# Second attention of a two-layer kernel: scores from three bf16 parts as six products in 64-row strips, operands stacked by 0/1 matmuls

## The chip, the cores and the metric

The kernel runs on one core of a Trainium2 chip. The metric is the device time of one execution in microseconds (us). TensorE (PE in the profile, PEld its weight loads) multiplies, VectorE (DVE), ScalarE (ACT) and GpSimd (POOL) do the rest, SyncE (SP) issues DMAs.

## The reference

Two layers, each an attention block and a feed-forward block with adaptive layer norm, on x of 1 x 2048 x 128. Only the second attention changes:

```python
q = (x @ Wqa @ Wqb).reshape(b, s, H, D)            # H = 16 heads, D = 8, s = 2048
kv = (x @ Wkva @ Wkvb).reshape(b, s, KVH, D, 2)    # KVH = 4 groups of keys and values
k, v = (kv[..., 0], kv[..., 1])
q = _rope(q); k = _rope(k)
k = jnp.repeat(k, g, axis=2); v = jnp.repeat(v, g, axis=2)
scores = jnp.einsum('bqhd,bkhd->bhqk', q, k) * scale
scores = jnp.where(causal[None, None], -jnp.inf, scores)
w = jax.nn.softmax(scores, axis=-1)
out = jnp.einsum('bhqk,bkhd->bqhd', w, v).reshape(b, s, E)
return out @ Wout + bout
```

## The kernel before

Each engine has its own program; semaphores join them. The 2048 tokens are four chunks c of 512 (`CW`), each four tiles of 128. The order in time is: first attention, routed experts, layer norm `norm(2)`, the second attention, `norm(3)`, the second experts.

**Operands.** A head has only 8 dimensions. To keep precision with bf16 matmuls, q and k are cut into three bf16 parts, and all nine products of parts are contracted at once: 9 x 8 = 72 rows (`KROWS`), plus two rows that subtract the row maximum, in a 128-row operand padded with zeros and ones. Per chunk the tensor engine makes latents (`latents`, L881 and L882), then q, k and v from them (`heads`, L888 to L895); the vector engine applies rope and splits (`rope_and_split`, L1726 to L1746: 14 operations); SyncE writes the parts to DRAM (`q_parts`, `k_parts`) and 18 DMAs per chunk read them back into the stacked form (`stack`, L482 and L485; chunks 2 and 3 from GpSimd's queue). Two GpSimd memsets fill the padding: L647 right after the first attention, L654 once the residual of the experts is added (`x2_ready`).

**Items and steps.** The work is 16 items n, one per chunk c = n // 4 and key group g (four heads). Two passes run over each item. The maxima pass makes scores with queries as rows, in "slots": a slot is one PSUM bank filled by TensorE (L927, and L930 and L931 for a diagonal tile and its mask) and read by a maximum on VectorE (L1766); banks 0, 1 and 7 rotate, so TensorE waits for the reader of three slots before. The main pass goes in steps (n, j), one per key tile j: 160 steps, 4, 8, 12 or 16 per item by chunk; the last four of each item are diagonal ones with fewer columns. A step is `sum_scores` for two pairs of heads (L968 to L971, transposed scores with the maximum subtracted), two exponentials on ScalarE (L1289) and `values` (L983, four fp32 matmuls side by side in 32 columns each), which runs one step behind. `attention_schedule` deals the slots out among the steps, so that an item's maxima are known before its first step; the slots of items 0 and 1 come before step 0. After an item VectorE copies its sum out (`copy_out`, L1754), and slots "out", "turned" and "product" finish it.

```python
                beside = SLOTS[s + 1]
                if j == 0:
                    pe.wait_ge(ld_nm[n % G1], 32 * (n // G1 + 1))
                cuts = [0, (len(beside) + 3) // 4, (len(beside) + 1) // 2, len(beside)]
                sum_scores(s, 0)
                for what in beside[cuts[0]:cuts[1]]:
                    slot(what)
                sum_scores(s, 1)
                for what in beside[cuts[1]:cuts[2]]:
                    slot(what)
                if s >= 1:
                    values(s - 1)
                for what in beside[cuts[2]:cuts[3]]:
                    slot(what)
```

## Time and profile before

| | us |
|---|---|
| median of 3 runs | 1316.51 (1315.25 to 1318.33) |
| profiled execution, span | 1317.5 |
| TensorE busy | 1166.7 (89%) |
| VectorE busy | 1046.4 (79%) |
| ScalarE busy | 776.6 (59%) |
| GpSimd busy | 43.9 (3%) |

The profile gives the profiled execution no other time than its span, from the first to the last instruction. It lies 1.0 us (0.08%) above the median. Busy shares are averages over stages with different limits, and matmuls overlap one another, so an engine's limit is read from the starts of its instructions in one stage.

### The profile page before, as it was taken

Reading aid. Unit: us, or ns where it says so; the run is one execution under the profiler, and the core shown is the slowest. Engines: PE = TensorE matmul, PEld = TensorE weight load, DVE = VectorE, ACT = ScalarE, POOL = GpSimd, SP = SyncE. Lnnn points to the kernel's source line nnn. Section 1 sums busy time; section 2 is a strip of 40 time slices with the busy share of each in tenths; the row PEclk is TensorE's granted clock in tenths of the full one; section 3 lists DMA queues with packets and bytes.
Section 4 is the critical chain, followed back from the end, with each engine's and each line's share of the span. In section 5 each row is a group of like instructions: output and inputs, shape, how many; then the busy total and the mean of one; then the engine's idle time right before and its main releaser. Section 6 shows DMA issues by size and latency. Waiting matters only on the chain.

```text
span 1317.5 us, 17710 instructions
## 1 busy us (share of the span) xinstructions
PE 1166.7 (89%) x6249; PEld 680.9 (52%) x6249; DVE 1046.4 (79%) x2018; ACT 776.6 (59%) x1151; POOL 43.9 (3%) x45
## 2 busy tenths in 40 slices
PE   3888647999999855779999999999998799999998
PEld 2333333666666512345444443443332688888886
DVE  4699998788888883879899889888851688888885
ACT  1635414899999710135555656566676566666664
POOL 0000020000000040140000000000000000000000
PEclk9898767899999956589999999999999699999999
DMA  5000000000000214551000000000000121111001
GB/s 161 0 0 1 0 24 17 16 17 16 18 14 1 78 35 79 72 78 16 2 2 2 1 1 2 1 1 1 1 1 1 45 102 56 56 56 56 0 1 33
DMA packets 38169, 35.02 MB, mean 27 GB/s; under 512 B 15162, under 2 KB 33530, under 8 KB 36810
## 3 DMA queue, kind: packets, MB, share of 16 engines
q1 hardware_dynamic: 36082, 31.12, 9.0%
q0 software_dynamic: 2016, 2.96, 1.7%
q8 instruction: 44, 0.72, 0.2%
q14 instruction: 27, 0.22, 0.1%
HBM read 30.85 MB, written 3.08 MB: 26 GB/s over the span
## 4 chain that ended last, share of the span: by engine, by line
PE 61%; DVE 26%; ACT 6%; issue 3%; DMA 3%; SPq 1%; DVEq 0%; ACTq 0%
PE ps L822 10%; PE ps L823 10%; PE ps L824 10%; PE ps L983 9%; DVE arena_a L1766 7%; PE ps L927 7%; PE ps L971 6%; DVE arena_b L1472 3%; DVE mv L1377 2%; PE ps L839 1%; ACT arena_b L1222 1%; DMA arena_a<-q_parts 1%; PE ps L693 1%; DMA arena_a<-arena_a 1%; DVE xn L1384 1%
## 5 line engine op out<-in xcount | busy, mean ns | idle before, releaser
L1766 DVE TENSOR_REDUCE arena_a<-ps 128x1 f32<-128x512 f32 (+3 forms) x560 | 344.4, 668 | 73.2 <-PE ps L931 46.3
L1289 ACT ACTIVATE arena_b<-ps 128x1024 f32<-128x1024 f32 (+3 forms) x320 | 274.0, 894 | 191.8 <-PE ps L971 169.6
L822 PE MATMUL ps<-parts 128*128 128x512 f32 x640 | 273.2, 427 | 7.1 <-DVE parts L1688 4.2
L823 PE MATMUL ps<-parts 128*128 128x512 f32 x640 | 251.5, 393 | 0.0
L824 PE MATMUL ps<-parts 128*128 128x512 f32 x640 | 251.2, 392 | 0.0
L927 PE MATMUL ps<-arena_b,arena_a 128*128 128x512 bf16 (+3 forms) x576 | 190.4, 354 | 6.3 <-DVE arena_a L1766 4.9
L971 PE MATMUL ps<-arena_a,arena_b 128*128 128x512 bf16 (+3 forms) x576 | 163.2, 348 | 0.7 <-ACT arena_b L1289 0.3
L983 PE MATMUL ps<-arena_b 128*32 128x512 f32 (+3 forms) x1280 | 151.1, 544 | 2.5 <-DVE arena_b L1754 2.2
L822 PEld LDWEIGHTS ps<-parts 128*128 128x128 f32 x640 | 122.0, 191 | 36.8 <-DVE parts L1688 9.7
L824 PEld LDWEIGHTS ps<-parts 128*128 128x128 f32 x640 | 121.0, 189 | 26.4
L823 PEld LDWEIGHTS ps<-parts 128*128 128x128 f32 x640 | 121.4, 190 | 22.4
L1867 DVE TENSOR_TENSOR arena_b<-ps,arena_b 128x512 f32<-128x512 f32 x128 | 88.3, 690 | 55.4 <-PE ps L824 51.6
L927 PEld LDWEIGHTS ps<-arena_b,arena_a 128*128 128x128 bf16 x576 | 52.8, 99 | 143.0 <-DVE arena_a L1766 119.0
L1312 ACT ACTIVATE arena_b<-ps 128x512 f32<-128x512 f32 x128 | 76.6, 599 | 84.5 <-PE ps L824 84.0
L1677 DVE TENSOR_TENSOR arena_b<-ps,arena_b 128x512 f32<-128x512 f32 x128 | 88.1, 689 | 35.2 <-ACT arena_b L1226 34.8
L1688 DVE TENSOR_TENSOR parts<-arena_b,parts 128x512 fp32r<-128x512 f32 x128 | 87.6, 685 | 1.2
L1872 DVE TENSOR_TENSOR parts<-arena_b,parts 128x512 fp32r<-128x512 f32 x128 | 87.3, 682 | 0.1
L1226 ACT ACTIVATE arena_b<-arena_b 128x512 f32<-128x512 f32 x128 | 80.7, 631 | 3.6
L1222 ACT ACTIVATE arena_b<-ps 128x512 f32<-128x512 f32 x128 | 74.9, 585 | 9.2 <-PE ps L824 9.1
L1316 ACT ACTIVATE parts<-arena_b 128x512 fp32r<-128x512 f32 x128 | 79.9, 624 | 0.4 <-DVE arena_b L1867 0.4
L971 PEld LDWEIGHTS ps<-arena_a,arena_b 128*128 128x128 bf16 x576 | 53.3, 99 | 35.0 <-ACT arena_b L1289 13.4
L930 PE MATMUL ps<-arena_b,arena_a 128*128 128x128 bf16 x256 | 53.8, 236 | 12.0 <-DMA arena_a<-q_parts 12.0
(274 smaller groups left out, 1445.3 us busy)
## 6 DMA issues: line engine op xcount, KB each, us to landing
arena_b<-expert_weights SPq DMA_DIRECT2D x7, 1024.0 KB, 6.7
arena_a<-q_parts SPq DMA_DIRECT2D x18, 128.0 KB
arena_a<-q_parts POOLq DMA_DIRECT2D x18, 128.0 KB, 5.9
wslot<-in_L_ffn_up_w SPq DMA_DIRECT2D x8, 256.0 KB, 3.1
wslot<-in_L_ffn_down_w SPq DMA_DIRECT2D x8, 256.0 KB, 3.3
wslot<-in_L_ffn_w_gate SPq DMA_DIRECT2D x8, 256.0 KB, 2.9
wslot<-in_L_ffn_w_up SPq DMA_DIRECT2D x8, 256.0 KB, 3.4
wslot<-in_L_ffn_w_down SPq DMA_DIRECT2D x8, 256.0 KB, 3.8
```

Of the source, the lines that this page charges most:

```text
L822: mm(bank, w(0), x(0), start=start, stop=False)
L823: mm(bank, w(0), x(1), start=False, stop=False)
L824: return mm(bank, w(1), x(0), start=False, stop=stop)
L927: last = mm(b[:, at_:at_ + full], q, kst[:, g, u * CW:u * CW + full], start=True, stop=True)
L971: last = mm(ps[:, 2 + i, full:CW], k, q[:, full:CW], start=True, stop=True)
L983: last = mm(ps[32 * i:32 * i + 32, 6, off:CW], vaug[:, j, g, :], probs[:, s % 2, i, off:CW], start=(j == 0), stop=(j == TPC * c + TPC - 1) ...
L1222: a(relu[:, k % NBUF, :], ps[:, k % 2, :], ACT.Relu).then_inc(moe_relu, 1)
L1289: a(probs[:, s % 2, 2 * pair:2 * pair + 2, off:CW], ps[:, 2 + 2 * pair:4 + 2 * pair, off:CW], ACT.Exp, scale=scale).then_inc(p2_exp, 1)
L1677: v.tensor_tensor(prod0[:, k % NBUF, :], ps[:, 2 + k % 2, :], sq0[:, k % NBUF, :], ALU.mult)\
L1688: v.tensor_tensor(hid0[:, k % NBUF, 1, :], prod0[:, k % NBUF, :], hid0[:, k % NBUF, 0, :].bitcast(F32), ALU.subtract).then_inc(moe_lo, 1)
L1766: v.tensor_reduce(mx[:, n % 2, i:i + fit, t % TPC, u], b[:, 0:fit * w].rearrange("p (h k) -> p h k", k=w), AX_X, ALU.max)\
L1867: v.tensor_tensor(prod1[:, k % NBUF, :], ps[:, 2 + k % 2, :], silg[:, k % 2, :], ALU.mult)\
```

## The change

- Six products of the nine are kept (`PRODUCTS`), so 48 rows and two for the maximum: 50 (`MROWS`). Two heads stand in one operand, in rows 0 to 49 and 64 to 113 (`STRIP` = 64), and each matmul of scores uses one strip.
- Projection weights are merged before the experts (`wq`, `wkv`): two transposes and two matmuls on TensorE, four copies on ScalarE. `queries`, `keys` and `values_all` take the normed x directly. All keys are roped and split once, four chunks in four bands of 32 partitions (`rope_k`).
- The DRAM trip is gone. A stacked operand is three matmuls by a 0/1 matrix (`stack`, L922) and a ScalarE copy (`stack_copy`, L1320 or L1322): 12 such before the first slot, 36 among the slots.
- Diagonal slots: instead of 11 slots per item on the diagonal, 12 ("diag" with one 512-column mask for four tiles, "below3", "below12").
- Both large GpSimd memsets are gone. GpSimd does the small weight copies and the bias addition on 128 x 2048 that VectorE did at L1718. `copy_out` moves to ScalarE. The maxima chain has one operation less.

```diff
+PRODUCTS = ((0, 0), (0, 1), (1, 0), (1, 1), (0, 2), (2, 0))
+KROWS = len(PRODUCTS) * HD
+MROWS = KROWS + 2
+STRIP = 64
...
+        blocks = [("scores", t, u) for t in range(TPC * c, TPC * c + TPC) for u in range(c)]
+        blocks += [("diag", 0, 0), ("below3", 0, 0), ("below12", 0, 0)]
+        for k, (what, t, u) in enumerate(blocks):
+            scores += [(what, n, t, u, i) for i in range(HPG)]
+            if c < NC - 1 and (len(blocks) - 1 - k) < HPG - 1:
+                scores.append(("stack", -1, c + 1, n % G1, k + HPG - 1 - len(blocks)))
...
-            nc.gpsimd.memset(kst[64:P, :, :], 1.0).then_inc(kones, 1)
-            nc.gpsimd.memset(qst[64:P].rearrange("p c h t -> p (c h t)").bitcast(F32), 0.0).then_inc(qzero, 1)
+            g.tensor_tensor(xt[:, :, :], xt[:, :, :], bo1[:, :].unsqueeze(1).broadcast_to([P, NT, D]), ALU.add)\
+                .then_inc(bias_ready, 1)
...
+            def stack(e, b):
+                c, g, kind = STACKS[e]
+                r = slice(0, P) if kind else slice(32 * c, 32 * c + 32)
+                for a in range(NPART):
+                    last = mm(b, spread[r, g, kind, a, :], (q3[:, c, a, :] if kind else k3[r, a, :]),
+                              start=(a == 0), stop=(a == NPART - 1))
+                return last
...
+                    r = slice(STRIP * (i % 2), STRIP * (i % 2) + KROWS)
+                    def pairs(at_, tq, k0, kw, stop=True):
+                        return mm(b[:, at_:at_ + kw], qst[r, g, tq // TPC, i // 2, tq % TPC * P:(tq % TPC + 1) * P], kst[r, g, k0:k0 + kw],
+                                  start=True, stop=stop, skip_group_check=not stop)
...
-                for i in (2 * pair, 2 * pair + 1):
-                    k = kst[:, g, j * P:(j + 1) * P]
-                    q = qst[:, c, HPG * g + i, :]
+                def part(i, lo, hi, stop):
+                    r = slice(STRIP * i, STRIP * i + MROWS)
+                    return mm(ps[:, 2 + 2 * pair + i, lo:hi], kst[r, g, j * P:(j + 1) * P],
+                              qst[r, g, c, pair, lo:hi], start=True, stop=stop)
...
+            keys(NC - 1)
+            queries(2)
+            stacks_before()
+            for what in SLOTS[0][:NITEM0]:
+                slot(what)
+            queries(3)
+            values_all()
+            for what in SLOTS[0][NITEM0:]:
+                slot(what)
...
+                    slots(beside[cut:] if pair else beside[:cut])
+                if s >= 1 and STEPS[s - 1][0] != n:
+                    copy_out(n - 1, s)
```

What stands on TensorE where the second attention begins, before the change: transposes of the norm (L674), then projections (L888 to L895 are `heads`, L881 and L882 `latents`), then the first slots.

```order
L674 MATMUL ps<-ident,xn 128x128 x4
L888 MATMUL ps<-arena_b,wqb 128x512
L889 MATMUL ps<-arena_b,wqb 128x512
L892 MATMUL ps<-arena_b,wkk 32x512
L893 MATMUL ps<-arena_b,wkk 32x512
L895 MATMUL ps<-wkk,arena_b 128x32 x4
L881 MATMUL ps<-hT,wqa 64x512
L882 MATMUL ps<-hT,wkva 32x512
```

And after it, from the third chunk's transposes on (L891 and L892 are `queries`, L897 and L899 `keys`, L922 `stack`, L961 and L974 a slot's scores and its mask):

```order
L675 MATMUL ps<-ident,xn 128x128 x4
L891 MATMUL ps<-hT,wq 128x512
L892 MATMUL ps<-hT,wq 128x512
L897 MATMUL ps<-hT,wkv 32x512
L899 MATMUL ps<-hT,wkv 32x512
L675 MATMUL ps<-ident,xn 128x128 x4
L897 MATMUL ps<-hT,wkv 32x512
L899 MATMUL ps<-hT,wkv 32x512
L922 MATMUL ps<-arena_a,arena_b 128x512 x36
L961 MATMUL ps<-arena_a 128x128 x4
L974 MATMUL ps<-maskqk,identb 128x512
```

The projections depend on nothing but the normed x now, and 36 stacking matmuls stand between them and the first slot.

A full step on TensorE, before (L971 `sum_scores`, L927 a slot, L983 `values`):

```order
L927 MATMUL ps<-arena_b,arena_a 128x512
L971 MATMUL ps<-arena_a,arena_b 128x512 x2
L927 MATMUL ps<-arena_b,arena_a 128x512 x2
L971 MATMUL ps<-arena_a,arena_b 128x512 x2
L927 MATMUL ps<-arena_b,arena_a 128x512
L983 MATMUL ps<-arena_b 32x512 x4
```

and after (L1010 `sum_scores`, L961 a slot, L1032 `values`):

```order
L961 MATMUL ps<-arena_a 128x512 x2
L1010 MATMUL ps<-arena_a 128x512 x2
L961 MATMUL ps<-arena_a 128x512
L1010 MATMUL ps<-arena_a 128x512 x2
L961 MATMUL ps<-arena_a 128x512
L1032 MATMUL ps<-arena_b 32x512 x4
```

The count is the same; each L1010 pair and each pair of neighbouring L961 now lies in different strips.

ScalarE in the first steps after the change (L1359 are the exponentials, L1320 and L1322 copies of stacked operands):

```order
L1359 ACTIVATE arena_b<-ps 128x1024
L1320 ACTIVATE arena_a<-ps 128x512
L1359 ACTIVATE arena_b<-ps 128x1024
L1359 ACTIVATE arena_b<-ps 128x2x384
L1322 ACTIVATE arena_a<-ps,onerow 128x512
L1359 ACTIVATE arena_b<-ps 128x2x384
L1359 ACTIVATE arena_b<-ps 128x2x256
L1320 ACTIVATE arena_a<-ps 128x512
```

Before, exponentials alone stood there; the copies come in between. Per item there are now 4, 3, 2, 1 stacks in chunk 0, 4, 4, 2, 2 in chunk 1 and 3, 3, 3, 0 in chunk 2.

## Rows read from the trace of the kernel before

**Rows 1.** The page: busy time by engine, share of the span, instructions.

```profile
PE 1166.7 (89%) x6249; PEld 680.9 (52%) x6249; DVE 1046.4 (79%) x2018; ACT 776.6 (59%) x1151; POOL 43.9 (3%) x45
```

**Rows 2.** Windows: busy time by engine (instructions), granted TensorE clock, DMA.

```profile
480.00:493.00 13.00, 12.54 (x23) 4.08 (x21) 7.86 (x13) 1.05 (x2) 0.00 (x0) 0.50 0.00 0
825.00:850.00 25.00, 24.87 (x193) 10.20 (x191) 21.94 (x41) 15.36 (x19) 0.00 (x0) 1.00 0.00 1
```

**Rows 3.** Timeline, GpSimd and VectorE: start, duration, operation, idle time before.

```profile
185.79 6.92 POOL L647 MEMSET arena_b<- 64x8192 bf16 x1 [184.95 <-DVE xt L1494]
187.09 5.65 DVE L1377 TENSOR_SCALAR mv<-mv 128x4 f32<-128x4 f32 x1
464.41 13.75 POOL L654 MEMSET arena_a<- 64x16384 f32 x1 [269.55 <-DVE xt L1494]
465.65 12.54 DVE L1377 TENSOR_SCALAR mv<-mv 128x4 f32<-128x4 f32 x1
480.63 2.29 DVE L1718 TENSOR_TENSOR xt<-xt,bo 128x2048 f32<-128x2048 f32 x1
```

**Rows 4.** Timeline of the start of the second attention.

```profile
464.79 1.97 PE L881 MATMUL ps<-hT,wqa 128*64 128x512 f32 x2
479.42 1.12 PE L674 MATMUL ps<-ident,xn 128*128 128x128 f32 x4 [10.82 <-DVE xn L1384]
482.34 1.91 PE L889 MATMUL ps<-arena_b,wqb 64*128 64x512 f32 x2
484.18 1.91 PE L892 MATMUL ps<-arena_b,wkk 32*32 32x512 f32 x2
485.88 1.91 PE L893 MATMUL ps<-arena_b,wkk 32*32 32x512 f32 x2
487.93 0.69 DVE L1726 TENSOR_TENSOR arena_b<-ps,arena_a 128x512 f32<-128x512 f32 x1 [5.00 <-PE ps L893]
495.24 0.67 DVE L1746 TENSOR_TENSOR arena_b<-arena_b 32x512 bf16<-32x512 f32 x1
523.90 0.27 PE L930 MATMUL ps<-arena_b,arena_a 128*128 128x128 bf16 x1 [11.99 <-DMA arena_a<-q_parts]
556.82 0.26 PE L968 MATMUL ps<-arena_a,arena_b 128*128 128x128 bf16 x1 [4.04 <-DVE arena_b L1729]
```

**Rows 5.** Timeline of one full step in chunk 2, on three engines.

```profile
828.10 1.06 PE L983 MATMUL ps<-arena_b 128*32 128x512 f32 x8
829.10 0.60 PE L927 MATMUL ps<-arena_b,arena_a 128*128 128x512 bf16 x2
829.52 2.48 DVE L1766 TENSOR_REDUCE arena_a<-ps 128x1 f32<-128x512 f32 x4 [0.48 <-PE ps L927]
829.54 0.59 PE L971 MATMUL ps<-arena_a,arena_b 128*128 128x512 bf16 x2
...
830.17 1.94 ACT L1289 ACTIVATE arena_b<-ps 128x1024 f32<-128x1024 f32 x2 [0.89 <-PE ps L971]
830.62 0.38 PE L927 MATMUL ps<-arena_b,arena_a 128*128 128x512 bf16 x1
830.92 1.06 PE L983 MATMUL ps<-arena_b 128*32 128x512 f32 x8
```

**Rows 6.** Timeline: `copy_out` after the last item of chunks 0 to 2, then items 14 and 15.

```profile
618.17 0.68 DVE L1754 COPY arena_b<-ps 128x512 f32<-128x512 f32 x1
711.21 0.68 DVE L1754 COPY arena_b<-ps 128x512 f32<-128x512 f32 x1
850.01 0.68 DVE L1754 COPY arena_b<-ps 128x512 f32<-128x512 f32 x1
980.80 0.69 DVE L1754 COPY arena_b<-ps 128x512 f32<-128x512 f32 x1 [3.83 <-PE ps L983]
1011.97 0.69 DVE L1754 COPY arena_b<-ps 128x512 f32<-128x512 f32 x1 [28.89 <-PE ps L983]
```

**Rows 7.** Groups by line: a ScalarE copy-like operation from PSUM, 512 columns.

```profile
L1312 ACT ACTIVATE arena_b<-ps 128x512 f32<-128x512 f32 x128 | 76.6, 599 | 84.5 <-PE ps L824 84.0
```

More of the change, by code:

```diff
@@ L78, in attention_schedule @@
     scores.append(("maxima", NITEM - 1))
-    end = {n: max(k for k, x in enumerate(scores) if x[1] == n and x[0] == "scores") + 1 for n in range(NITEM)}
+    end = {n: max(k for k, x in enumerate(scores) if x[1] == n and x[0] != "maxima") + 1 for n in range(NITEM)}
     slots = [scores[:end[1]]]
@@ L414, in adaln_two_layers, with slot_before @@
         STEPS, SLOTS, LAST_SLOTS = attention_schedule()
-        FIRST = [SLOTS[0][:len(SLOTS[0]) // 2], SLOTS[0][len(SLOTS[0]) // 2:]]
         NFIRST = len(SLOTS[0])
+        PRE = 3 * G1
+        STACKS = [(c, g, kind) for c in range(NC) for g in range(G1) for kind in range(3)]
         def slot_bank(m):
             return m % 2 if m < NFIRST else (0, 1, 7)[m % 3]
-        def slot_free(m):
-            return m - 1 if m < NFIRST else max(NFIRST, m - 2)
-        READ = {what: m + 1 for m, what in enumerate([x for part in SLOTS for x in part] + LAST_SLOTS)}
+        ORDER = [x for part in SLOTS for x in part] + LAST_SLOTS
+        READ = {}
+        for what in ORDER:
+            READ[what] = 1 + sum(1 for x in READ if (x[0] == "stack") == (what[0] == "stack"))
+        def slot_before(m):
+            same = [k for k in range(m) if slot_bank(k) == slot_bank(m)]
+            return ORDER[same[-1]] if same else None
+        NITEM0 = min(k for k, x in enumerate(SLOTS[0]) if x[1] == 1 or x[0] == "maxima")
         HALF = GP * NC
@@ L899, in after_turn, with stacks_before @@
             def after_turn(c):
-                if c >= 2:
-                    heads(c - 2)
                 if c >= 1:
-                    latents(c - 1)
+                    if c <= 2:
+                        queries(c - 1)
+                    keys(c - 1)
+            def stack(e, b):
[5 more added lines that the diff above has]
+                return last
+            def stacks_before():
+                pe.wait_ge(ld_e, 16)
+                pe.wait_ge(ksplit_ready, 1)
+                for e in range(PRE):
+                    if e == 1:
+                        pe.wait_ge(split_ready, 1)
+                    if e >= 2:
+                        pe.wait_ge(stack_ready, e - 1)
+                    stack(e, ps[:, 6 + e % 2, :]).then_inc(stack_mm, 1)
             slot_at = [0]
@@ L961, in sum_scores @@
                     pe.wait_ge(p2_exp, 2 * s + pair - 1)
[L962 to L971 removed]
+                full = off + P if j >= TPC * c else off
+                def part(i, lo, hi, stop):
+                    r = slice(STRIP * i, STRIP * i + MROWS)
+                    return mm(ps[:, 2 + 2 * pair + i, lo:hi], kst[r, g, j * P:(j + 1) * P],
+                              qst[r, g, c, pair, lo:hi], start=True, stop=stop)
+                if full > off:
+                    for i in range(2):
+                        part(i, off, full, False)
+                    for i in range(2):
+                        last = mm(ps[:, 2 + 2 * pair + i, off:full], identb[:, :], maskkq[:, :], start=False, stop=True)
+                if full < CW:
+                    for i in range(2):
+                        last = part(i, full, CW, True)
                 last.then_inc(p2_mm, 1)
@@ L1749, in copy_out, with rope_q @@
-            def copy_out(n, steps):
-                dve.wait_ge(pv_mm, steps)
-                if n >= 2:
-                    dve.wait_ge(slot_read, READ["out", n - 2])
-                v.tensor_copy(oT[:, n % 2, :], ps[:, 6, :]).then_inc(o_copy, 1)
+            chain(v.memset(mx, -BIG))
+            dve.wait_ge(ld_rope, 48)
+            def rope_q(c):
+                b, bank = c % 2, 4 - 2 * (c % 2)
+                dve.wait_ge(q_mm, c + 1)
+                if c == 1:
+                    dve.wait_ge(ksplit_ready, 1)
+                elif c >= 2:
+                    dve.wait_ge(split_ready, c - 1)
+                v.tensor_tensor(ra[:, b, :], ps[:, bank, :], ropec[:, chunk(c)], ALU.mult).then_inc(rope_done, 1)
+                v.tensor_tensor(rb[:, b, :], ps[:, bank + 1, :], ropes[:, chunk(c)], ALU.mult).then_inc(rope_done, 1)
+                dve.wait_ge(rope_done, 2 * c + 2)
+                chain(v.tensor_tensor(ra[:, b, :], ra[:, b, :], rb[:, b, :], ALU.add))
+                split(q3[:, c], ra[:, b, :]).then_inc(split_ready, 1)
```

418 lines of the change are left out of this document (210 added, 208 removed).

## The prediction, as it was put on record

> **What bounds the kernel now.** The page first: TensorE is busy 89% of the span, VectorE 79% [rows 1]. Only the stretch from about 456 to 1013 us belongs to the second attention, so I read the windows of it next. From 825 to 850 TensorE shows 24.87 of 25 us, VectorE 21.94, ScalarE 15.36, at full clock (2.4 GHz); from 480 to 493, at the start, the clock is at half (1.2 GHz), VectorE is busy 7.86 of 13 us and ScalarE 1.05 [rows 2]. Two stages, then, with different limits.
>
> **The steps.** The timeline of one full step settles what limits them [rows 5]. `values` starts at 828.10 and again at 830.92: 2.82 us per step. In between TensorE never stops: 1.00 us for `values`, then eight bf16 matmuls of 512 columns (four slots, four of `sum_scores`) from 829.10 to 830.62 for seven of them, 0.217 us each, and 0.30 us from the start of the last to the next `values`, that is 0.085 beyond its 0.217. VectorE needs 2.48 us for four maxima and then waits (0.48 before); ScalarE needs 1.94 and waits 0.89. TensorE is the bound, VectorE is next at 88% of the step, ScalarE third at 69%.
>
> **The start.** The timelines of GpSimd and VectorE, side by side, show an operation on 4 elements, L1377, lasting 12.54 us while GpSimd's memset L654 runs, and ending with it (478.19 against 478.16); its twin at 187.09 lasts 5.65 us beside L647 [rows 3]. Unhindered it takes 0.17. After it comes a chain through projection, rope, store and reload: TensorE's first slot waits 11.99 us for `q_parts`, and the first step begins at 556.82 [rows 4].
>
> **The change part by part.** The sum is made against the profiled 1317.5 us, which is the median within 0.1%.
>
> *First memset gone:* 5.65 - 0.17 = -5.5 us. This VectorE chain feeds the routing before the experts, and TensorE waits for it, so it counts in full. Bounds -4 (six small GpSimd copies now come there; they are priced by nothing here) and -7. The merging of weights falls where TensorE and ScalarE wait for the routing on VectorE: nothing; without that cover some 4 us.
>
> *The start anew*, from 465.7 us, where L1377 stalled. It now passes in 0.17, so the 12.4 us is part of what follows. TensorE needs (at half clock, as rows 4 show for such matmuls) three times `queries` and four times `keys`, with the transposes of two chunks between them (1.1 us, L674). L889 to L892 gives 1.84 us for a matmul, L892 to L893 1.70. From 464.8: queries 3.7, keys 3.4, transposes 1.1, queries 3.7, keys 3.4, transposes 1.1, keys twice 6.8, together 23.2: 488.0. `rope_k` is half of the 14 operations between 487.93 and 495.91 [rows 4], 4.1 us: 492. Rope of q0 lies under the projections, that of q1 under the stacks. The bias addition on GpSimd (2.29 us on VectorE at L1718) blocks, if it blocks like a memset, operations that wait for keys anyway: nothing. Twelve stacks are 36 matmuls: at half clock 0.43 each, 15.5 us; at full clock the two banks and the copy (0.60, [rows 7]) bind, about 0.85 per stack, 10: 502 to 507.5. First slots (12 and 3 stacks): VectorE 12 x 0.6 = 7, or TensorE cold 11: 510 to 518.5. The last queries, rope of q2 and `values_all` are waited for one after another: 8 to 12: 518 to 530. Second slots 8 to 10, rope of q3 until its banks are read 1.3: step 0 begins between 527 and 541.5 against 556.8 in the trace. I take the middle, -23 us, bounds -15 and, with TensorE warm from 480 on, -34.
>
> *The steps.* Four terms per step, if two matmuls in different strips run together:
> - `sum_scores`, full step: four matmuls become two pairs: 0.87 - 0.43 = -0.43 us.
> - A diagonal step gains as much less by its columns, but its masks need all 128 rows, so a pair of heads goes from strips to the full array and back. A change of form is read off `values`: 0.085 us in, and 1.00 - 4 x 0.217 = 0.13 in and out together with its drain, so about 0.09. The gain in a diagonal step is eaten by this: nothing.
> - A full slot is still one matmul; only neighbours in different strips can overlap. A "diag" slot gets two changes of form, +0.2 us, four per item.
> - A stack slot adds 3 x 0.217 + 0.2 = 0.85 us on TensorE, 36 of them 31 us, on ScalarE 0.60, 36 of them 22, none on VectorE.
>
> A full step then is 1.09 + 0.43 + 4 x (0.11 to 0.217) = 1.95 to 2.4 us on TensorE, 2.4 to 2.48 on VectorE, 1.94 on ScalarE. VectorE becomes the bound at 2.45: -0.38 per full step. By chunks, against the copy-outs [rows 6]:
> - Chunk 3, 162 us: 36 full steps with slots by 0.38 = -14; item 15 without slots goes from TensorE (31.2 us) to ScalarE, 1.94 per full step against 2.09: -2; -17 with a `copy_out` less on VectorE.
> - Chunk 2, 138.8 us: 32 full steps, -12, nine stacks displace as much VectorE work as they add: -11.
> - Chunk 1, 93.0 us: 16 full steps would give -6, but 12 stacks (10 us) and 16 "diag" slots fall on TensorE: 24 to 29 us per item against 23.3: +5.
> - Chunk 0, 61.4 us from step 0, with an item and a half under cold clock and a late reload: TensorE 57: -3.
>
> Together -26 us. Bounds: -50 if changes of form cost nothing and neighbours always overlap, +15 if strips don't run together.
>
> *Sum:* -5.5 - 23 - 26 = -54.5, so 1317.5 - 54.5 = **1263 us**.
>
> The Trainium skill has a rule against this. Its page "TensorEngine Tiling (Array Packing)", section Tiling Modes, says that changing the mode, not only the tile, drains the array. The row agrees: 0.085 us into `values`; the other way, the page "TensorE: Matmul & The Clock Gate" (Part 2) puts a drain at about 128 cycles, by my estimate 0.053 us, and over some 450 changes of form the sum would be about 15 us lower. The first page also says that row tiles work in parallel, which no row here shows.
>
> **The rivals.**
> 1. *Strips don't overlap.* Nothing in the trace has two matmuls in different row strips. Then full steps stay at 2.82, and stacks (31 us) and diag slots (16 x 0.8) load TensorE where chunks 0 and 1 have no slack: +10 to +15 on the steps instead of -26: 1300 us. Chance 0.14.
> 2. *Slower than before: the clock falls.* The granted clock was at half from 480 to 493 [rows 2] while TensorE worked without a pause in matmuls of 64*128 and 32*32, 1.84 and 1.70 us each [rows 4]; it was at full in the stage of 128*128 and four-wide `values` [rows 2]. The new steps use 50 rows per matmul. At half clock a full step costs 2.0 + 0.17 + 0.87 + 0.9 = 3.9 us on TensorE, 1.1 above now; 96 of them +105, diagonal ones +1 each, +64, minus 34 at the start: about 1450. It decides once it holds in a fifth of the steps. Against it: `values` fills its four column strips at once and takes 41% of the step. Chance 0.07.
> 3. *Stacks stall the slots.* A bank with a stack is free only when ScalarE, in its order, has passed an exponential and copied. TensorE queues everything behind it: `sum_scores`, `values`. At 0.5 to 0.9 us for each of 36, 18 to 32 us: 1288. For: ScalarE's order ties copies to exponentials. Against: it is idle 31% of a step. Chance 0.13.
> 4. *Better than forecast:* full clock from the start and cheap changes of form, -34 and -50: about 1228. Chance 0.12.
>
> **How the numbers follow.** The forecast (1240 to 1280) has 0.54. The range holds 1, 3 and most of 4: 1230 to 1300; outside are 0.07 for rival 2 and about 0.12 at the two ends. A measurement of this kernel tells 0.2% (2.6 us) from no change. Slower: rival 2, and 0.01 for others, 0.08; the same 0.02; faster 0.90.
>
> **What would show it.** L1377 at 0.17 us in both norms. Step 0 begins 61 to 76 us after the third L1377 of `norm(2)`, not 91. Starts of an L1010 pair a few ns apart, in full steps 2.45 us from one L1032 to the next, with VectorE gapless and TensorE waiting for it. Chunk 1 no faster than before. The prediction is wrong if L1010 starts are 0.217 apart (rival 1), if the granted clock is below 1.00 in the steps (rival 2), or if TensorE waits for L1320 (rival 3).

## The result, and the profile after

The changed kernel takes **1297.78 us** (median of four, 1295.01 to 1299.13) against 1315.88 (1310.24 to 1318.33) beside it: ratio 0.9885, 95% interval 0.9842 to 0.9927. The direction is as forecast. The time is inside the range (1230 to 1300) by 2.2 us, and that is luck: a start that came earlier than forecast stands against steps that came out longer. Of the 54.5 us forecast, 18.1 are there between the medians and 24.3 between the profiled spans (1317.5 and 1293.2). The spans are used below because only a profile can be split into stages; that of before, 1317.5, is above the median of its times even without what a time holds beyond the span, so it is one of its longer executions. In the page, VectorE lost and ScalarE gained; TensorE did not lose anything [rows 1]:

```profile
PE 1171.0 (91%) x6178; PEld 626.5 (48%) x6191; DVE 1010.3 (78%) x1975; ACT 808.4 (63%) x1208; POOL 8.0 (1%) x14
```

Timeline of the changed kernel, from the first norm after the first layer to the first step (start, duration, engine, line, operation; in brackets the idle time before it and what ended it):

```profile
186.74 0.53 DVE L1451 TENSOR_SCALAR mv<-mv 128x4 f32<-128x4 f32 x1
...
458.87 0.17 DVE L1451 TENSOR_SCALAR mv<-mv 128x4 f32<-128x4 f32 x1
...
461.58 4.52 POOL L658 TENSOR_TENSOR xt<-xt,bo 128x2048 f32<-128x2048 f32 x1 [272.89 <-DVE xn L1458]
...
463.13 3.52 DVE L1794 TENSOR_TENSOR arena_b<-arena_b 128x512 f32<-128x512 f32 x1
...
476.00 0.74 PE L922 MATMUL ps<-arena_a,arena_b 32*128 32x512 bf16 x2 [2.66 <-DVE arena_a L1802]
...
519.81 0.29 PE L1010 MATMUL ps<-arena_a 50*128 50x128 bf16 x2 [2.63 <-issue]
```

L1451 is the old L1377. It takes 0.53 and 0.17 us where it took 5.65 and 12.54 [rows 3]: both memset stalls are gone, but for 0.36 us of the first, which ended together with a GpSimd memset of 1.80 us that was left in (L637, 185.44 to 187.24). From the third L1451 of the norm to step 0 it is 519.81 - 458.87 = 60.9 us, forecast 61 to 76, before 91.2. Step 0 begins 37.0 us earlier than at 556.82 [rows 4], forecast 28.5 with the first memset. The first part did better than forecast.

The steps did not. ScalarE's `copy_out` after the last item of chunks 0 to 3:

```profile
584.85 0.60 ACT L1348 ACTIVATE arena_b<-ps 128x512 f32<-128x512 f32 x1
...
687.26 0.60 ACT L1348 ACTIVATE arena_b<-ps 128x512 f32<-128x512 f32 x1
...
835.69 0.60 ACT L1348 ACTIVATE arena_b<-ps 128x512 f32<-128x512 f32 x1
...
987.80 0.60 ACT L1348 ACTIVATE arena_b<-ps 128x512 f32<-128x512 f32 x1 [0.55 <-PE ps L1032]
```

Against [rows 6], from step 0 on, in us:

| chunk | before | forecast | after | 64-row strips (below) |
|---|---|---|---|---|
| 0 | 61.4 | 58 | 65.0 | 63.6 |
| 1 | 93.0 | 98 | 102.4 | 102.3 |
| 2 | 138.8 | 128 | 148.4 | 132.4 |
| 3 | 162.0 | 145 | 152.1 | 152.0 |
| all | 455.2 | 429 | 468.0 | 450.4 |

So the steps take 13 us more than before instead of 26 less; -37 + 13 = -24 is the whole change. A full step in chunk 3 is what the forecast said (timeline of TensorE, then of the other two engines):

```profile
891.90 1.06 PE L1032 MATMUL ps<-arena_b 128*32 128x512 f32 x8
892.90 0.39 PE L961 MATMUL ps<-arena_a 48*128 48x512 bf16 x2
893.13 0.38 PE L1010 MATMUL ps<-arena_a 50*128 50x512 bf16 x2
893.38 0.39 PE L961 MATMUL ps<-arena_a 48*128 48x512 bf16 x1
893.38 0.60 PE L1010 MATMUL ps<-arena_a 50*128 50x512 bf16 x2
894.07 0.39 PE L961 MATMUL ps<-arena_a 48*128 48x512 bf16 x1
894.39 0.64 PE L1032 MATMUL ps<-arena_b 128*32 128x512 f32 x4
```

```profile
890.84 7.46 DVE L1826 TENSOR_REDUCE arena_b<-ps 128x1 f32<-128x512 f32 x12
...
891.07 1.94 ACT L1359 ACTIVATE arena_b<-ps 128x1024 f32<-128x1024 f32 x2 [0.55 <-PE ps L1010]
```

From L1032 to L1032 it is 2.49 us; "x2 0.38" means that two matmuls of 512 columns began and ended as one, so strips run together; VectorE does twelve maxima without a pause. What is new stands in the windows of the same kernel (busy time and instructions of TensorE, weight loads, VectorE, ScalarE, GpSimd, then the granted clock as a share of 2.4 GHz):

```profile
573.70:687.20 113.50, 109.39 (x867) 36.26 (x868) 100.39 (x204) 68.29 (x90) 0.00 (x0) 1.00 0.01 2
687.20:705.00 17.80, 17.68 (x74) 5.22 (x74) 9.19 (x19) 7.34 (x9) 0.00 (x0) 0.52 0.00 1
705.00:729.00 24.00, 23.53 (x191) 7.60 (x188) 20.88 (x41) 15.89 (x20) 0.00 (x0) 1.00 0.01 2
...
764.00:780.00 16.00, 15.67 (x67) 4.42 (x68) 6.82 (x16) 6.19 (x7) 0.00 (x0) 0.50 0.00 1
804.00:808.00 4.00, 4.00 (x20) 1.18 (x19) 2.52 (x7) 0.88 (x2) 0.00 (x0) 0.57 0.00 0
808.00:987.80 179.80, 173.06 (x1353) 49.07 (x1349) 132.74 (x252) 132.78 (x152) 0.00 (x0) 1.00 0.01 1
```

In chunk 2 the clock stands at half (1.2 GHz) for some 37 us, in three stretches (688 to 705, 763 to 780, 804 to 807). TensorE is busy for 17.68 of the 17.80 us of the first, with 74 matmuls: it did not fall because the engine waited. In the ten us before the fall it was as busy, at full clock:

```profile
678.00:687.90 9.90, 9.76 (x83) 2.89 (x79) 9.65 (x17) 5.95 (x10) 0.00 (x0) 1.00 0.00 0
```

The timeline at its edge shows only half-speed matmuls in place of full-speed ones, in the first steps of item 8:

```profile
687.18 0.60 PE L1010 MATMUL ps<-arena_a 50*128 50x512 bf16 x2
687.77 1.20 PE L961 MATMUL ps<-arena_a 48*128 48x512 bf16 x2
688.38 1.02 PE L1010 MATMUL ps<-arena_a 50*128 50x512 bf16 x2
```

In the kernel before, every window of chunks 1 to 3 shows 1.00; this is its chunk 2:

```profile
711.20:850.00 138.80, 137.49 (x1039) 57.29 (x1035) 123.92 (x239) 84.20 (x97) 0.00 (x0) 1.00 0.01 1
```

### The profile page after: what moved, and what is told of

Read it like the earlier page. It is cut to its first block, busy times and chain, and to the rows that moved or that the text cites. A ratio compares the mean times of both kernels' runs of the same rounds, so it can differ in the third digit from the quotient of the medians.

```text
span 1293.2 us, 17992 instructions
## 1 busy us (share of the span) xinstructions
PE 1171.0 (91%) x6178; PEld 626.5 (48%) x6191; DVE 1010.3 (78%) x1975; ACT 808.4 (63%) x1208; POOL 8.0 (1%) x14
## 4 chain that ended last, share of the span: by engine, by line
PE 65%; DVE 24%; ACT 7%; issue 3%; DMA 0%; SPq 0%; ACTq 0%; DVEq 0%
PE ps L831 10%; PE ps L832 10%; PE ps L833 10%; PE ps L1032 9%; PE ps L961 7%; DVE arena_b L1826 7%; PE ps L1010 4%; PE ps L922 3%; DVE arena_b L1546 3%; PE ps L974 2%; PE ps L1017 1%; PE ps L848 1%; ACT arena_b L1278 1%; PE ps L694 1%; ACT arena_b L1359 1%
## 5 line engine op out<-in xcount | busy, mean ns | idle before, releaser
L1359 ACT ACTIVATE arena_b<-ps 128x1024 f32<-128x1024 f32 (+3 forms) x320 | 275.0, 895 | 151.0 <-PE ps L1010 129.0
L1826 DVE TENSOR_REDUCE arena_b<-ps 128x1 f32<-128x512 f32 x384 | 237.5, 681 | 12.3 <-PE ps L961 10.8
L961 PE MATMUL ps<-arena_a 48*128 48x128 bf16 (+3 forms) x832 | 186.2, 321 | 11.2 <-DVE arena_b L1826 3.2
L1032 PE MATMUL ps<-arena_b 128*32 128x512 f32 (+3 forms) x1280 | 157.3, 565 | 0.0
L1010 PE MATMUL ps<-arena_a 50*128 50x512 bf16 (+3 forms) x832 | 151.1, 317 | 5.3 <-issue 2.6
L961 PEld LDWEIGHTS ps<-arena_a 48*128 48x128 bf16 x832 | 60.4, 97 | 183.4 <-DVE arena_b L1826 113.4
L1828 DVE TENSOR_REDUCE arena_b<-ps 128x4 f32<-128x512 f32 x64 | 43.5, 691 | 35.0 <-PE ps L974 34.9
L1010 PEld LDWEIGHTS ps<-arena_a 50*128 50x128 bf16 x832 | 42.8, 94 | 55.0 <-ACT arena_b L1359 23.2
```

Of the source, the lines that this page charges most:

```text
L961: return mm(b[:, at_:at_ + kw], qst[r, g, tq // TPC, i // 2, tq % TPC * P:(tq % TPC + 1) * P], kst[r, g, k0:k0 + kw], start=True, stop=sto ...
L1010: return mm(ps[:, 2 + 2 * pair + i, lo:hi], kst[r, g, j * P:(j + 1) * P], qst[r, g, c, pair, lo:hi], start=True, stop=stop)
L1032: last = mm(ps[32 * i:32 * i + 32, 6, off:CW], vaug[:, j, g, :], probs[:, s % 2, i, off:CW], start=(j == 0), stop=(j == TPC * c + TPC - 1) ...
L1359: a(probs[:, s % 2, 2 * pair:2 * pair + 2, off:CW], ps[:, 2 + 2 * pair:4 + 2 * pair, off:CW], ACT.Exp, scale=scale).then_inc(p2_exp, 1)
L1826: v.tensor_reduce(m8[:, t % TPC, 4 + u:5 + u], b, AX_X, ALU.max).then_inc(slot_read, 1)
```

## The experiments

Theory A: the clock is lost because the steps' matmuls use few rows of the array. Rival B: rows don't matter, something else does (the order, the waits, chance). Beside it: what the second memset, the strips' overlap, the masks and the stacks are each worth. The medians below also hold what varies outside the steps: step 0 began between 514.0 and 526.8 us in the changed kernel and its variants, and what follows the last `copy_out` took 302.3 to 306.6 us. So where a part of the steps is priced, it is by the lengths of chunks in the profiles, one profile each.

**1. The kernel before without the second memset** (no rows of zeros are needed if scores contract rows 0 to 71 and sums 0 to 73).

```
-            nc.gpsimd.memset(qst[64:P].rearrange("p c h t -> p (c h t)").bitcast(F32), 0.0).then_inc(qzero, 1)
...
-                        q = qst[:, t // TPC, HPG * g + i + h, t % TPC * P:(t % TPC + 1) * P]
+                        q = qst[0:KROWS, t // TPC, HPG * g + i + h, t % TPC * P:(t % TPC + 1) * P]
...
-                    k = kst[:, g, j * P:(j + 1) * P]
+                    k = kst[0:KROWS + 2, g, j * P:(j + 1) * P]
```

> The kernel before without GpSimd's second long memset (that of qst, L654): scores contract rows 0 to 71 and the sums rows 0 to 73, so no zero rows are needed. Theory: the memset held the VectorE instruction of the last norm (L1377) for some 12 us and everything behind it, so the time falls by 10 to 13 us to about 1304 us, step 0 begins 10 to 13 us earlier, and the steps are as before, at full clock. Rival: the transfers that stack the parts set the start of step 0 anyway; then it gains under 4 us (1312 us or more).

Measured: 1305.64 us against 1311.13, ratio 0.9955 (0.9922 to 0.9988). Step 0 began at 546.0, 10.8 us earlier than in the first trace of before; chunk 0 then took 63.8 us, not 61.4. Less than half of the 12.4 us stall comes through to the median. That lies between theory and rival. Where the rest went, the old start's transfers or the longer chunk 0, one profile each doesn't settle. The clock stood at 1.00 from 580 us to the end of the steps, with 72 and 74 rows.

**2 and 3. All rows.** Slots alone, then slots and sums, contract all 128 rows, so that a score is the sum of two heads' scores.

```
-                    r = slice(STRIP * (i % 2), STRIP * (i % 2) + KROWS)
+                    r = slice(0, P)
...
-                    r = slice(STRIP * i, STRIP * i + MROWS)
+                    r = slice(0, P)
```

> The changed kernel with the score slots (L961) contracting all 128 rows, so that each score is the sum of two heads' scores; the sums of the steps (L1010) stay in strips. Theory A: the clock falls because too little of the array works in 48-row matmuls; then there are no half-clock stretches at 688, 763 and 804 us (granted clock 1.00 in all steps), worth some 17 us, less 3 to 8 us for slots that no longer overlap the other strip's work: 1283 to 1292 us. Theory B: the number of rows does not matter; then the stretches stay and the time is 1298 to 1306 us.

> The changed kernel with score slots and sums (L961, L1010) contracting all 128 rows, so every score is a sum over two heads; nothing overlaps by strips. Price of the strips: a full step is 2.83 us as in the kernel before against 2.49 us. Theory A (few rows cost the clock): the clock is 1.00 in all steps, and the time is 1300 to 1312 us (the strips' gain lost, the clock's loss back). Theory B (rows do not matter): half-clock stretches as in the changed kernel, 1318 to 1332 us.

Measured: 1308.19 us (1298.70 to 1310.57) and 1282.73 us (1281.38 to 1290.35), beside before at 1311.13. Windows of the run with slots and sums, chunks 1, 2 and 3:

```profile
571.30:673.70 102.40, 100.64 (x767) 44.09 (x779) 89.72 (x181) 62.13 (x81) 0.00 (x0) 1.00 0.01 1
673.70:814.70 141.00, 138.00 (x989) 55.80 (x1007) 115.86 (x222) 90.63 (x111) 0.00 (x0) 1.00 0.01 1
814.70:978.10 163.40, 158.64 (x1114) 57.05 (x1130) 108.55 (x205) 114.41 (x131) 0.00 (x0) 1.00 0.00 1
```

In both the half-clock stretches of chunks 1 to 3 are gone, as theory A says. Both times lie outside what I expected, though, on either side. A kernel in which nothing overlaps was 15 us faster by its median than the changed one; in the profiles it is 11.7, of which 5.8 are an earlier step 0 (514.0) and 3.8 the steps (464.2 against 468.0). Mixing 128-row slots with strips was slower than either (chunk 1 in 108.5 us, chunk 3 in 165.3).

**4. Both heads of a pair in one strip** (heads 1 and 2 of a group change places in the output).

```
-                    r = slice(STRIP * i, STRIP * i + MROWS)
+                    r = slice(STRIP * pair, STRIP * pair + MROWS)
...
-                              qst[r, g, c, pair, lo:hi], start=True, stop=stop)
+                              qst[r, g, c, i, lo:hi], start=True, stop=stop)
```

> The changed kernel with the two heads of a pair of sums (L1010) taken from one strip of rows, so that they queue instead of overlapping (heads 1 and 2 of each group change places in the output). Theory: the pair's matmuls start 0.22 us apart, a full step is 2.7 to 2.85 us instead of 2.49, and the time is 1312 to 1330 us; the half-clock stretches stay or grow fewer if the clock follows how densely the array works. Rival: overlap across strips is worth little since VectorE sets the steps: under 5 us.

Measured: 1296.77 us once and 1316.53 to 1318.86 three times, in the profile chunk 3 in 168.6 us and six half-clock stretches (from 732, 770, 811, 845, 896 and 981 us). The profile is of an execution of 1318.08 us, and the four times lie too far apart, so neither the overlap nor the clock is judged by it; experiment 14 does that.

**5 and 6. All rows with the right result.** Two copies of the stacked keys, each with zeros in the other strip's rows; then the same with strips in chunk 3.

```
-        kst = take([G1, T], BF16)
+        kst = take([2, G1, T], BF16)
...
-                    a(kst[:, g, chunk(c)], ps[:, bank, :], ACT.Identity, bias=onerow[:, :]).then_inc(stack_ready, 1)
+                    for h in range(2):
+                        last = a(kst[:, h, g, chunk(c)], ps[:, bank, :], ACT.Identity,
+                                 bias=onerow[:, h:h + 1], scale=onerow[:, 2 + h:3 + h])
+                    last.then_inc(stack_ready, 1)
```

> The changed kernel with two copies of the stacked keys, each with zeros in the other strip's rows, written by ScalarE (one more 0.6 us copy for each of 16 stacks of keys); all scores and sums contract 128 rows, and the output is the reference's. Theory A (the clock holds when all rows are in use, zeros included, since the kernel before with 128 rows and zeros from row 74 held it): granted clock 1.00 in the steps, 1283 to 1292 us, as the run with all rows and two heads' sums. Theory B (it was the data and not the rows: zeros do not count): half-clock stretches again, over 1300 us.

> As the run before, but the items of chunk 3 (12 to 15) go in strips of 48 and 50 rows, as in the changed kernel; chunks 0 to 2 contract 128 rows. Theory: chunk 3 takes 152 us as in the changed kernel (163 with all rows), chunk 2 about 142 us with no half-clock stretch: 1272 to 1282 us, the fastest so far. Rival: changing between 128-row and 48-row matmuls while chunk 2's steps run beside chunk 3's scores costs what the strips give: 1285 us or more.

Measured: 1293.71 us (1292.64 to 1297.73) and 1290.60 us (1285.11 to 1297.64), before 1315.72. Both lie above what theory A gave in time. With zeros in half of the rows the clock is at 1.00 from 526 us to the end of the steps, so zeros do as well as data here. With strips of 48 and 50 rows in chunk 3, stretches came back just there (at half from 879 to 886 and from 961 to 964), and chunk 3 took 156.1 us, not 152: theory A is borne out in the clock. The rival, that mixing 48-row slots into chunk 2's 128-row steps costs time, is borne out too: chunk 2 took 145.5 us at full clock, against 141.5 in experiment 5.

**7. One 0/1 matmul per late stack** (two of three parts are left out in chunks 1 to 3): `stack(e, b, 1)` in a slot.

> The changed kernel with one 0/1 matmul in place of three for each of the 36 late stacks (two of three parts are left out in chunks 1 to 3). Theory: 72 matmuls of 512 columns at 0.217 us are 15.6 us of TensorE, most of them on its path in chunks 0 to 2, so these take 10 to 16 us less; chunk 1 takes 97 to 98 us instead of 102. Rival: ScalarE's copies, not the matmuls, are what the stacks cost: under 4 us. For the clock: if fewer matmuls that use all rows are left, the half-clock stretches of chunk 2 stay or grow.

Measured: 1282.68 us (1281.22 to 1290.37). That is 15.1 less than the changed kernel's first median, as the theory says, but step 0 began 4.2 us later and there were four half-clock stretches in the steps (from 683, 720, 788 and 867 us, the last in chunk 3), so it prices nothing. Chunk 1 took 99.0 us at full clock; the cleaner price is in experiment 13.

**8. Slots of 50 rows.** `r = slice(STRIP * (i % 2), STRIP * (i % 2) + MROWS)` for L961.

> The changed kernel with the score slots contracting 50 rows in place of 48, as the sums do (the two more rows are zero in the queries at that time, so nothing changes in the result). Theory C: part of what the strips give is eaten by changes of form between 48 and 50 rows, six per step; with one form the steps of chunk 1 take 1 to 4 us less and the total is 1285 to 1294 us. Rival: the form change is that of strip or dtype, not of the number of rows: within 0.2% of the changed kernel (1295 to 1300 us).

Measured: 1286.59 us (1281.18 to 1296.41). The time is inside theory C's range, but not for its reason. Chunk 1 took 104.5 us, not less than 102.4, and chunk 3 152.0, so the step is no cheaper. The profiled spans differ by 14.0 us, all of it in the steps, and the clock was at half there for 10 us of chunks 1 to 3 (640 to 647, 790 to 793) where it was for 37 in the changed kernel. The 11 us between the medians lie within what the changed kernel itself spreads over (experiment 10).

**9 and 10. Strips of 64 rows, and the changed kernel again beside it.** Rows 48 or 50 to 63 of the queries' strip are zeros from the stack's 0/1 matmul, so the result is the same.

```
-                    r = slice(STRIP * (i % 2), STRIP * (i % 2) + KROWS)
+                    r = slice(STRIP * (i % 2), STRIP * (i % 2) + STRIP)
...
-                    r = slice(STRIP * i, STRIP * i + MROWS)
+                    r = slice(STRIP * i, STRIP * i + STRIP)
```

> The changed kernel with scores and sums contracting all 64 rows of their strip in place of 48 and 50; the added rows are zero in the queries, so the result is the same, and the overlap of strips stays. Theory A (rows in use, zeros included, hold the clock; 128 rows held it, 72 rows in the run without the memset too): fewer or no half-clock stretches in the steps, full steps still 2.49 us, 1275 to 1288 us. Theory D (it is the overlapping pairs, or the 64-row form itself, that the clock does not count): stretches of 20 us and more in all as in the changed kernel, 1290 to 1300 us.

> The changed kernel itself, beside the run with 64 rows and for the run with 50 rows. If the half-clock stretches are a matter of chance from one execution to the next, their places and sum differ from the first profile (688 to 705, 763 to 780, 804 to 807 us), and the times spread over 10 us or more; then the 11 us between the 50-row run and the changed kernel are chance too. If they are fixed by the instructions, they stand where they stood and the times keep to 1295 to 1300 us.

Measured: **1277.57 us** (1275.21 to 1280.28), ratio to before 0.9744 (0.9700 to 0.9788); the changed kernel beside it 1294.67 us (1288.39 to 1300.46), 0.9865 (0.9814 to 0.9916). The same stretches of time as above, with 64 rows:

```profile
583.70:686.00 102.30, 98.56 (x777) 32.54 (x780) 89.66 (x181) 62.23 (x80) 0.00 (x0) 1.00 0.01 1
686.00:705.00 19.00, 18.39 (x128) 6.61 (x129) 14.59 (x34) 12.91 (x16) 0.00 (x0) 1.00 0.00 1
705.00:818.50 113.50, 111.32 (x878) 33.63 (x880) 100.12 (x189) 77.73 (x96) 0.00 (x0) 1.00 0.01 2
818.50:970.50 152.00, 145.72 (x1132) 40.83 (x1130) 107.78 (x205) 114.03 (x131) 0.00 (x0) 1.00 0.01 1
```

From 686 to 705 us TensorE gets 128 matmuls done, where it got 74 from 687.2 to 705. Step 0 began at the same time to 0.3 us, and chunks 1 and 3 are as long as in the changed kernel to 0.1 us; chunk 2 differs by 16.0 and chunk 0 by 1.4. The second profile of the changed kernel had half-clock stretches at 585 to 595, 694 to 705, 766 to 783 and 807 to 811 us: near the old places, with one more and other lengths. Its chunks 1 and 2 took 106.3 and 146.1 us:

```profile
586.40:692.70 106.30, 102.72 (x777) 33.40 (x780) 89.44 (x181) 62.17 (x80) 0.00 (x0) 0.96 0.01 1
692.70:838.80 146.10, 143.14 (x1005) 42.90 (x1009) 115.22 (x222) 90.97 (x111) 0.00 (x0) 0.89 0.01 1
```

So the stretches belong to this kernel, but their places and sum vary, and the times spread over 12 us (5 with 64 rows).

**11 and 12. No causal masks**, first on the changed kernel, then on that with 64-row strips (L974 and L1017 left out, so later keys are not masked).

> The changed kernel without the causal masks (L974 and L1017, 64 and 128 pairs of matmuls' worth: scores of later keys are not masked). Theory: the matmuls that the masks take (64 of 512 columns, 256 of 128) and the changes of form around them are what diagonal steps cost beyond the forecast; 64 x 0.22 + 256 x 0.054 = 28 us of columns and some 250 changes of 0.09 us = 22 us, of which half falls where TensorE is the bound: 20 to 30 us less outside clock effects, the steps around each item's end falling from 2.7 to 2.3 us. Rival: VectorE bounds these steps too; under 8 us less.

> The run with 64-row strips without the causal masks (L974 and L1017; scores of later keys are not masked). Theory: masks and the changes of form around them are why diagonal steps of chunk 3 are 0.36 us longer than in the kernel before; without them chunk 3 takes 147 to 149 us in place of 152.0 and chunk 1 some 96 us in place of 102.3, if the clock is at 1.00. Rival: VectorE or ScalarE bound those steps; chunk 3 at 151 us or more, chunk 1 at 100 or more. For theory A on the clock: with fewer 128-row matmuls half-clock stretches may come back.

Measured: 1279.72 us (1268.73 to 1284.02) with 50 rows, 1244.49 us (1242.03 to 1247.13) with 64. With 50 rows there were eight half-clock stretches in the steps from 570 us on: taking the 128-row mask matmuls away made the clock worse. With 64 rows one short one was left, from 910 to 914 us, and the price of the masks can be read: 33 us in all against the run with masks, 7.0 in chunk 1, 7.7 in chunk 2, 7.0 in chunk 3. Another 9.9 are in chunk 0, where the clock also came back to full sooner (at 528 us, not 535), so that part is not the masks alone.

**13. One matmul per late stack, 64 rows.**

> The run with 64-row strips with one 0/1 matmul per late stack in place of three (two of three parts are left out in chunks 1 to 3). Theory: 72 matmuls of 0.217 us, so chunk 1 takes 102.3 - 24 x 0.217 = 97 us, chunk 0 some 5 us less, chunk 2 some 2 to 4 less; the total 1263 to 1268 us. Rival: ScalarE's copies are what is waited for: chunk 1 at 101 us or more, total 1274 us or more.

Measured: 1270.18 us (1262.21 to 1270.31), 7.4 less for 72 matmuls; chunk 1 in 100.0 us with one short half-clock stretch at 636 us, chunk 2 in 129.4, chunk 3 unchanged. Step 0 began 4.0 us earlier (five late stacks stand before it). Chunk 0 was 2.0 longer, with the clock at half until 548 us. Half of the 15.6 us does not show in the total; neither theory's number was met.

**14. Both heads of a pair in one strip, 64 rows.**

> The run with 64-row strips with both heads of a pair of sums (L1010) in one strip (heads 1 and 2 of each group change places in the output). Theory: each pair then takes 0.22 us more, so where VectorE does not cover it the steps take up to 0.43 us more: chunk 3 at 163 to 168 us in place of 152, chunk 2 at 138 to 146 in place of 132, total 1295 to 1310 us. Rival: overlap of pairs is worth under 5 us in all, and the gain in full steps came from elsewhere.

Measured: 1295.49 us (1292.73 to 1298.48). Chunk 1 103.9 us, chunk 2 133.4, chunk 3 160.6: without the pairs' overlap they take 1.5, 0.9 and 8.6 us more, and chunk 0 takes 2.1 more, 13 in all. Chunk 3 has one half-clock stretch in it, from 957 to 960 us. The chunks stay below what the theory gave them. The total is in its range only because step 0 began 5.3 us later, with the clock at half from 475 to 492 us, in a stage that the edit does not touch. The two pairs of one full step (timeline of TensorE):

```profile
891.80 0.59 PE L1010 MATMUL ps<-arena_a 64*128 64x512 bf16 x2
892.05 0.39 PE L961 MATMUL ps<-arena_a 64*128 64x512 bf16 x1
892.28 0.59 PE L1010 MATMUL ps<-arena_a 64*128 64x512 bf16 x2
```

"x2 0.59" is two matmuls 0.21 us apart where "x2 0.38" stood at 893.13. The Trainium skill, page "TensorE: Matmul & The Clock Gate", Part 3, says that matmuls placed in different tiles of the array run concurrently. The traces agree: 0.38 us for a pair in two strips, 0.59 for a pair in one.

**15 and 16. Fewer changes between strips and the full array.** In the diag slots of heads 0 and 2 the mask comes first; then also the sums of a diagonal step in one matmul.

```
+                        if first:
+                            m()
                         for k in range(TPC):
+                            last = pairs(k * P, TPC * c + k, c * CW + k * P, P, stop=first, start=not first)
+                        if not first:
+                            last = m()
```

> The run with 64-row strips; in every other diag slot (heads 0 and 2) the mask's matmul comes first and the four of the strip behind it, so that the masks of heads 1 and 2 are neighbours. The columns are the same; at most 32 changes into the full array and back go, of about 0.1 us each way. If changes of form are what the masks cost beyond their columns: 3 to 6 us less in the steps, 1271 to 1275 us. If only columns count, or if sums stand between the slots anyway: within 2 us of the run with 64 rows (1276 to 1280 us).

> As the run before, and in a diagonal step the sums of a head are one matmul over all its columns, with the mask behind it, in place of three (diagonal block, mask, rest): 192 matmuls fewer and one change from the full array back to a strip fewer inside the pair. If changes and starts count: another 4 to 9 us less, 1263 to 1271 us. If only columns count: the same as the run before.

Measured: 1280.60 us (1279.53 to 1281.09) and **1273.09 us** (1267.18 to 1276.13), ratio 0.9703 (0.9650 to 0.9756). From step 0 to the last `copy_out` the steps take 448.5 and 446.7 us against 450.4: each edit is worth 1.9 and 1.8 us there, of which 1.3 and 0.9 are in chunks 1 to 3. Both times lie above what was expected, and the gain in the steps is below it (3 to 6 and 4 to 9 us). Otherwise the two differ in the start (step 0 at 524.2 and 516.7 us): the clock stood at half from 475 to 492 us in the first, and only to 477 and again from 491 in the second. The last is the fastest version that leaves nothing out.

## Why the prediction was wrong in its size

**First memset: right.** 0.53 for 5.65 us is -5.1, forecast -5.5; the 0.36 us that are left ended with the memset L637, before the first of the small copies (187.40), and no VectorE operation is held beside those.

**Start anew: right in kind, too small.** 60.9 us from L1451 to step 0 gives, with -6.8 us up to L1451, -37.0 where -28.5 was forecast. The step "at half clock, as rows 4 show for such matmuls" was off: the clock was 1.00 from 463 to 476, where the projections ran, and the first stack began 17.1 us after L1451, not 26.3. (The forecast's sum counts two of its three `queries`; the third, from 471.36, lay beside `rope_k` and cost nothing.) The clock was 1.00 from 480 to 492 too, and the 36 stack matmuls took 10.8 us (476.0 to 486.8), the forecast's own figure at full clock (10). From 494 to step 0 it was 0.57, and these 33.0 us from the last stack matmul lie at the upper end of the forecast's 25 to 34. The result lies inside the bound for a warm start (-34). Experiment 1 bounds what the second memset has in this: without it the old kernel's step 0 began 10.8 us earlier, and its median was under 6 lower. The rest of the 30.2 us (37.0 - 6.8, forecast 23) is the rebuilt start.

**Strips overlap: right.** Rival 1 is out: full steps of 2.49 us (forecast 2.45), VectorE without a pause. But experiment 14 shows what the overlap of L1010's pairs is worth: 13 us in all, 8.6 of them in chunk 3 and 2.4 in chunks 1 and 2 together. What strips give in all, with the overlap of slots and less the changes of form that 128 rows everywhere do without, is experiment 3 against 9 at full clock: nothing in chunk 1, 8.6 us in chunk 2 and 11.4 in chunk 3, together 20. The start, not the strips, carries the gain: even with 64 rows the steps take 450.4 us against 455.2 before.

**The step that failed: the clock.** The sum used full clock in all steps and left rival 2 at 0.07, with the remark that it "decides once it holds in a fifth of the steps". It held in less, 18 us of chunk 0 and some 37 of chunk 2, an eighth of the steps. In chunk 2 it cost 16.0 us (148.4 against 132.4 with 64 rows), the largest single part of the 39 us by which the steps missed. In chunk 0 it was at half from 504 to 538 us; the run with all 128 rows, at full clock from 520, took 57.3 us for that chunk, forecast 58, measured 65.0: another 7, of which 64 rows gave back only 1.4. These are the rows, of the changed kernel first:

```profile
503.60:537.80 34.20, 29.00 (x131) 9.62 (x132) 17.55 (x33) 9.91 (x13) 0.00 (x0) 0.50 0.00 1
...
520.00:571.30 51.30, 49.26 (x455) 25.36 (x461) 42.51 (x95) 28.24 (x44) 0.00 (x0) 1.00 0.01 2
```

The other runs say the same: with 5.4 us of chunk 0 at half clock it took 58.2 us (experiment 5), with 14.5 us 63.6 (9), with 22.3 us 66.6 (10). Together the clock is 23 of the 39. The argument against the rival, "`values` fills its four column strips at once and takes 41% of the step", was not enough: `values` was there all the time.

The Trainium skill, page "TensorE: Matmul & The Clock Gate", Part 1, ties the clock to how busy TensorE has been. No idle time explains these rows: 17.68 us busy of 17.80 at 0.52. What goes with it is the number of rows: with 48 and 50 rows in strips (the changed kernel twice, experiments 7, 8, 11, chunk 3 of 6) there were half-clock stretches in the steps of chunks 1 to 3; with 72, with 128 in all or in the slots alone, and with 128 of which half are zeros, none; with 64, none in experiments 9, 15 and 16 and one under 4 us each in 12, 13 and 14. Three pairs of kernels differ in the rows alone: 9 and 10, 7 and 13, 11 and 12; the half-clock time in chunks 1 to 3 falls from 39.8, 37.5 and 60.5 us to 0, 3.4 and 3.4. So that more rows bring the clock back is shown for chunks 1 to 3; by what measure the chip decides is not. Few rows alone are not enough for a fall either: chunks 1 and 3 of the changed kernel's first profile are at 1.00 with the same 48 and 50 rows. A second condition is visible but was not tested. In chunks 1 to 3 the three falls of this profile come 0.7, 1.2 and 2.1 us after an item's `copy_out` (687.26, 761.81, 801.93), that is behind its diagonal steps with few columns, and so, within 0.3 to 2.1 us, do all but one of the falls in these chunks in experiments 6 to 8, 10 and 11. With 64 rows the items end in the same way and the clock stays.

**The rest of the steps, some 16 us.** Chunk 3 (+7), chunk 1 (+4), chunk 2 (+4, by its time with 64 rows). Much of it is one place that the forecast costed in chunk 1 only: the four "diag" slots of an item. In one step of chunk 3 of the changed kernel:

```profile
899.69 1.06 PE L1032 MATMUL ps<-arena_b 128*32 128x512 f32 x8
900.69 0.39 PE L961 MATMUL ps<-arena_a 48*128 48x128 bf16 x4
901.02 0.39 PE L974 MATMUL ps<-maskqk,identb 128*128 128x512 bf16 x1
901.34 0.39 PE L961 MATMUL ps<-arena_a 48*128 48x128 bf16 x4
901.66 0.39 PE L974 MATMUL ps<-maskqk,identb 128*128 128x512 bf16 x1
901.99 0.39 PE L1010 MATMUL ps<-arena_a 50*128 50x512 bf16 x2
902.22 0.39 PE L961 MATMUL ps<-arena_a 48*128 48x128 bf16 x4
902.53 0.39 PE L974 MATMUL ps<-maskqk,identb 128*128 128x512 bf16 x1
902.86 0.39 PE L1010 MATMUL ps<-arena_a 50*128 50x512 bf16 x2
903.08 0.33 PE L961 MATMUL ps<-arena_a 48*128 48x384 bf16 x1
903.34 1.06 PE L1032 MATMUL ps<-arena_b 128*32 128x512 f32 x8
```

Each diag slot holds TensorE for 0.65 us (900.69 to 901.34), and up to four of them fall into one step. This step, with three, takes 3.65 us, not 2.49, and the one before, with the fourth, 2.82: 1.5 us for this item's scores. Where two and two share a step it is 2.99 us twice, 1.0. Three items' scores lie in chunk 3 and four in chunk 2: by that some 4 and 5 us, an estimate from these rows. The masks' columns were there before too, but spread over slots and steps. The changes of form themselves (forecast 0.09 us) are 0.11 here: a diag slot takes 0.65 where its 1024 columns need 4 x 0.053 + 0.217 = 0.43. Experiments 15 and 16 took out some of them and got 3.7 us back. The "diagonal step gains nothing" held nearly: four such steps of item 13 take 2.82, 2.74, 2.63 and 2.29 us (from 907.89), 10.5 together, and 10.9 before. What remains, about 2 us in chunk 3 and the 4 in chunk 1, I have not separated. In chunk 1 the step from 606.17, with all four diag slots, takes 4.17 us. Experiment 13 says that stacks' matmuls are not fully on the path there (2.4 us for 24 of them, whose columns take 5.2), and 12 that masks are (7.0).

**Rival 3, stacks stall the slots: no.** Longest waits of TensorE from step 0 on (us in total, times, longest):

```profile
PE ps L961 <- DVE arena_b L1826: 3.2, 14, 0.4
...
PE ps L961 <- ACT arena_a L1322: 0.6, 2, 0.3
...
PE ps L961 <- ACT arena_a L1320: 0.4, 2, 0.2
```

1.0 us in all for the copies of stacks, where 18 to 32 was feared.

## What to carry to other kernels

When a change makes matmuls narrower in rows, check the granted clock in the windows of the new steady state before counting its overlap as a gain: here it cost 16 us in a chunk where the strips give 8.6, and contracting rows that hold zeros, at no time of its own, brought it back. Price an operation that changes the array's form where several of it fall into one step, not only by its sum. And an experiment that prices a part is only clean when the clock is the same on both sides: experiments 4, 7 and 11 gave no price, their likes with 64 rows (14, 13 and 12) did. Even then the price is read from the stage that the edit touches, since step 0 moved by 7.5 us between experiments 15 and 16, whose instructions before it are the same.

## What the runs showed of the hardware beyond that

- GpSimd's addition on 128x2048 held a VectorE addition of two SBUF inputs: L1794 took 3.52 us in place of 0.69, until L658 ended (461.58 + 4.52 = 466.10, against 463.13 + 3.52 = 466.65). VectorE additions that read PSUM beside it (L1791, at 461.81) took 0.69. The forecast had this case as "blocks like a memset" and priced it at nothing, which held.
- 128-row slots between 50-row sums (experiment 2) cost more than 128 rows everywhere (experiment 3): 146.7 against 141.0 us in chunk 2 and 108.5 against 102.4 in chunk 1, all at full clock.
- The start comes in two forms: the clock at half, or at full, from 480 to 488 us, and step 0 at 520 to 527 or at 514 to 520. Experiments 9 and 14 have the same instructions up to there and differ (520.1 and 525.4). Only the changed kernel has two profiles (both at full, 519.8), so whether a kernel keeps to one form is not shown, and what decides it is open.
